# Output projection and feed-forward of the first graph layer, written out with two or three buffers and statistics made per group

## The reference, cut to what matters

```python
h_attn = (wV / (z + 1e-06)).reshape(N, D_MODEL)   # N = 6250, D_MODEL = 128, 8 heads
x = h_attn @ Wo.T + bo
x = h + x
x = _batch_norm(x, bn1_w, bn1_b)                  # mean and variance over the 6250 nodes
y = relu(x @ W1.T + b1) @ W2.T + b2               # 128 -> 256 -> 128
y = x + y
y = _batch_norm(y, bn2_w, bn2_b)
```

## Time and profile before

| | us |
|---|---|
| median of 3 runs | 5488.98 |
| lowest and highest of them | 5485.43, 5491.85 |
| the profiled execution, its own time | 5493.95 |
| span of its trace, first to last instruction | 5492.1 |
| from the first instruction of `attend_out` (1312.48) to the end of its groups (1378.3) | 65.8 |
| its statistics and scale (1379.1 to 1389.2) | 10.1 |
| from the first instruction of `feed_forward` (1390.50) to the end of its groups (1467.2) | 76.7 |
| its statistics and scale (1467.3 to 1477.3) | 10.1 |

### The profile page before, as it was taken

How to read it: one execution, slowest core, us unless ns; L and a number is a source line. 1 busy time by engine, 2 the same in 40 slices (tenths; PEclk the granted TensorE clock), 3 DMA queues, 4 the chain that set the end, 5 groups by cost and what they waited for, 6 DMA issues and landing times. The chain is left out here.

```text
span 5492.1 us, 99934 instructions
## 1 busy us (share of the span) xinstructions
PE 4376.5 (80%) x24072; PEld 3667.3 (67%) x24073; DVE 3581.9 (65%) x7941; ACT 2266.5 (41%) x4134; POOL 2777.4 (51%) x2730
## 2 busy tenths in 40 slices
PE   7566667666567777777648848999999999999998
PEld 4455555554234444444347738999999999999998
DVE  4888888886478888888786675444445654443444
ACT  0333443332135555555426644444444443344333
POOL 0477777773047777777412103444444443344433
PEclk8788888887887777877779959999999999999999
DMA  1444444442157777777425534343434442233332
GB/s 46 121 117 117 118 117 116 117 116 81 33 168 198 198 200 197 199 198 198 136 65 158 154 84 163 141 151 143 149 141 161 173 151 106 101 135 144 138 125 94
DMA packets 543152, 750.77 MB, mean 137 GB/s; under 512 B 57967, under 2 KB 441966, under 8 KB 542734
## 3 DMA queue, kind: packets, MB, share of 16 engines
q1 hardware_dynamic: 461182, 521.35, 28.4%
q0 software_dynamic: 81552, 224.63, 15.4%
HBM read 584.36 MB, written 161.41 MB: 136 GB/s over the span
## 5 line engine op out<-in xcount | busy, mean ns | idle before, releaser
L544 POOL DMA_INDIRECT arena<-table_kv,arena x1664 | 1732.7, 1041 | 653.1 <-issue 505.2
L2288 PE MATMUL ps<-moving,parts 128*128 128x384 f32 (+1 forms) x11662 | 2015.8, 331 | 38.5 <-ACT moving L2350 20.4
L2288 PEld LDWEIGHTS ps<-moving,parts 128*128 128x128 f32 x11662 | 1949.5, 188 | 72.1 <-ACT moving L2350 29.3
L2229 POOL CAST moving<-counts 128x1152 fp32r<-128x1152 uint8 (+1 forms) x420 | 476.2, 1134 | 737.9 <-PE ps L2288 606.4
L340 ACT ACTIVATE counted<-ps 128x392 uint8<-128x392 f32 x1568 | 665.0, 503 | 333.7 <-PE ps L331 300.3
L2229 POOL CAST moving<-big 128x1152 fp32r<-128x1152 uint8 (+1 forms) x413 | 468.6, 1135 | 610.1 <-PE ps L2288 610.1
L331 PE MATMUL ps<-by_place,by_lo 128*128 128x392 bf16 x1568 | 631.2, 525 | 105.3 <-DVE by_place L295 74.2
L654 PE MATMUL ps<-arena 128*128 128x137 f32 x1664 | 321.3, 349 | 344.6 <-DVE arena L788 332.5
L2350 ACT ACTIVATE moving<-counts 128x1152 fp32r<-128x1152 uint8 (+1 forms) x360 | 366.9, 1024 | 436.0 <-PE ps L2288 433.0
L2350 ACT ACTIVATE moving<-big 128x1152 fp32r<-128x1152 uint8 (+1 forms) x354 | 360.4, 1023 | 429.7 <-PE ps L2288 429.6
L654 PEld LDWEIGHTS ps<-arena 128*128 128x128 f32 x1664 | 273.1, 239 | 374.0 <-ACT arena L699 222.5
(11 more groups left out here) (329 smaller groups left out, 5337.3 us busy)
## 6 DMA issues: line engine op xcount, KB each, us to landing
counts<-adjacency SPq DMA_DIRECT2D x53, 2352.0 KB, 8.5
big<-adjacency SPq DMA_DIRECT2D x52, 2352.0 KB, 8.6
adjacency<-slots SPq DMA_DIRECT2D x784, 98.0 KB
edge_values<-arena SPq DMA_DIRECT2D x208, 256.0 KB
arena<-edge_values SPq DMA_DIRECT2D x208, 256.0 KB, 3.3
arena<-table_kv,arena POOLq DMA_INDIRECT x1664
big<-table_norm SPq DMA_DIRECT2D x60, 192.0 KB, 5.7
big<-adjacency SPq DMA_DIRECT2D x7, 1568.0 KB, 6.6
```

What stands on the lines that cost most here:

```text
L544: pool.indirect_dma_start(m.ring4[r][:, k * 2 * D:(k + 1) * 2 * D], None, table, bass.IndirectOffsetOnAxis(m.src[:, j * HALF + k:j * HALF ...
L2229: pool.tensor_copy(to, of).then_inc(by_pool, 1)
L2288: mm = pe.matmul(m.bank(g % 2, n * P), d.parts[SOURCE[u]][:, s + q, t_, :], moving[:, q * n * P:(q + 1) * n * P], start=(s + q == 0 and t_ ...
```

## The change

`attend_out` and `feed_forward` no longer loop on the engines: the 7 groups are written out.

In `attend_out`, weight sums get their 1e-6 and reciprocal in one instruction each for all 49 blocks (`z` now lies in `m.prod`). The input, the scaled rows, their transpose and both PSUM areas have two buffers each (group g uses banks 0 to 3 or 4 to 7). The multiplication (`weigh`) and the transposes (`turn`) of groups 0 and 1 are issued ahead of the loop, and those of group g+2 inside step g: on VectorE ahead of the wait for group g's product, on TensorE behind group g's product. The degrees move from behind the groups to between `weigh(1)` and step 0.

In `feed_forward` the normed input has three buffers, each half of the hidden layer two in SBUF (and one pair of banks in PSUM), the product two pairs of banks. ScalarE issues the norm of group g+2 behind the ReLU of group g; TensorE issues the hidden layer of group g+1 ahead of the product of group g; VectorE issues its ReLU of group g+1 ahead of the last step of group g.

`batch_stats` is split: `piece_stats` makes, behind each group's last step, the statistics of those 250-node pieces which that group completes (3, 4, 3, 4, 3, 4 and 4 of them), and `batch_scale` keeps the rest.

The diff, with removed lines left out where the kernel above shows them:

```diff
@@ -1413,14 +1413,28 @@
     act.activation(root, two[:, :, 1], ACT.Sqrt, bias=m.eps[:, 0:1]).then_inc(rooted, 1)
 
 
...
+PIECE = 250
+assert NODES % PIECE == 0
+def pieces(g):
+    return range(g * GN // PIECE, min((g + 1) * GN, NODES) // PIECE)
+def piece_stats(dve, m, g, done, stats):
+    six = m.small[:, 0:6 * (NODES // PIECE)].rearrange("p (b n) -> p b n", n=6)
+    dve.wait_ge(done, g + 1)
+    for b in pieces(g):
+        op = dve.bn_stats(six[:, b, :], m.feat[:, b * PIECE:(b + 1) * PIECE])
+    op.then_inc(stats, 1)
+def batch_scale(dve, m, stats, weight, bias, rooted, scaled):
+    dve.wait_ge(stats, GROUPS)
+    dve.bn_aggr(m.mean_var, m.small[:, 0:6 * (NODES // PIECE)]).then_inc(stats, 1)
     dve.wait_ge(rooted, 1)
     dve.reciprocal(m.scale, m.scale).then_inc(scaled, 1)
     dve.wait_ge(scaled, 1)
@@ -1433,102 +1447,150 @@
 
 def batch_root(act, m, stats, rooted):
 
...
+    act.wait_ge(stats, GROUPS + 1)
     act.activation(m.scale, m.mean_var[:, 1:2], ACT.Sqrt, bias=m.eps[:, 0:1]).then_inc(rooted, 1)
 
 
 def attend_out(nc, m, t):
 
 
...
+    with Phase(nc, "ao0", "x_in0 x_in1 added inverted weighed turned copied out done degs rooted2 stats rooted scaled") as (
+            block, x_in0, x_in1, added, inverted, weighed, turned, copied, out, done, degs, rooted2, stats, rooted, scaled):
+        x_in = (x_in0, x_in1)
+        x = [m.stage_c[:, k * GN:(k + 1) * GN] for k in range(2)]
+        mean = [m.stage_a, m.stage_b]
+        mean_t = [m.ring4[k][:, 0:GN] for k in range(2)]
+        sums = blocks(m.sums[:, 0:BLOCKS * A0], A0)
+        z = blocks(m.prod[:, 0:BLOCKS * H0], H0)
 
         @block.sync
         def _(sp):
...
+            for g in range(GROUPS):
+                wait(sp, done, g - 1)
+                sp.dma_start(x[g % 2], t["xT"][:, g * GN:(g + 1) * GN]).then_inc(x_in[g % 2], 16)
 
         @block.vector
         def _(dve):
...
+            def weigh(g):
+                wait(dve, turned, g - 1)
+                b = slice(g * GB, (g + 1) * GB)
+                dve.tensor_tensor(blocks(mean[g % 2]).rearrange("p b (n c) -> p b n c", c=C0),
+                                  sums[:, b, 0:D].rearrange("p b (n c) -> p b n c", c=C0), copies(z[:, b, :], 3, C0),
+                                  ALU.mult).then_inc(weighed, 1)
+            dve.tensor_scalar(z, sums[:, :, D:D + H0], 1e-6, None, ALU.add).then_inc(added, 1)
+            dve.wait_ge(added, 1)
+            dve.reciprocal(z, z).then_inc(inverted, 1)
+            dve.wait_ge(inverted, 1)
+            weigh(0)
+            weigh(1)
+            dve.tensor_scalar(m.degree[:, :], sums[:, :, A0 - 1], 1.0, None, ALU.add).then_inc(degs, 1)
             dve.wait_ge(rooted2, 1)
             dve.reciprocal(m.norm[:, :], m.norm[:, :]).then_inc(degs, 1)
...
+            for g in range(GROUPS):
+                if g + 2 < GROUPS:
+                    weigh(g + 2)
+                dve.wait_ge(out, g + 1)
+                dve.wait_ge(x_in[g % 2], 16 * (g // 2 + 1))
+                dve.scalar_tensor_tensor(m.feat[:, g * GN:(g + 1) * GN], m.ps[:, 2048 * (g % 2) + 1024:2048 * (g % 2) + 1024 + GN],
+                                         m.column["bo"], x[g % 2], ALU.add, ALU.add).then_inc(done, 1)
+                piece_stats(dve, m, g, done, stats)
+            batch_scale(dve, m, stats, m.column["n1w"], m.column["n1b"], rooted, scaled)
 
         @block.tensor
         def _(pe):
...
+            def turn(g):
+                pe.wait_ge(weighed, g + 1)
+                wait(pe, copied, g - 1)
+                turn_blocks(pe, m, 4 * (g % 2), mean[g % 2]).then_inc(turned, 1)
+            turn(0)
+            turn(1)
+            for g in range(GROUPS):
                 pe.wait_ge(copied, g + 1)
...
+                wait(pe, done, g - 1)
+                feature_product(pe, m, 4 * (g % 2) + 2, [(m.w["wo"][:, 0, :], mean_t[g % 2])]).then_inc(out, 1)
+                if g + 2 < GROUPS:
+                    turn(g + 2)
 
         @block.scalar
         def _(act):
...
+            def copy(g):
                 act.wait_ge(turned, g + 1)
...
+                wait(act, out, g - 1)
+                act.activation(mean_t[g % 2], m.ps[:, 2048 * (g % 2):2048 * (g % 2) + GN], ACT.Copy).then_inc(copied, 1)
+            copy(0)
             act.wait_ge(degs, 1)
...
+            act.activation(m.norm[:, :], m.degree[:, :], ACT.Sqrt).then_inc(rooted2, 1)
+            for g in range(1, GROUPS):
+                copy(g)
             batch_root(act, m, stats, rooted)
 
 
 def feed_forward(nc, m):
 
 
...
+    with Phase(nc, "ff0", "normed hidden0 hidden1 relu0 relu1 out done stats rooted scaled") as (
+            block, normed, hidden0, hidden1, relu0, relu1, out, done, stats, rooted, scaled):
+        x = [m.stage_a, m.stage_b, m.stage_d[:, 0:GN]]
+        act0 = [m.ring4[k][:, 0:GN] for k in (0, 1)]
+        act1 = [m.ring4[k][:, 0:GN] for k in (2, 3)]
 
         @block.scalar
         def _(act):
...
+            def norm(g):
+                wait(act, done, g - 2)
+                act.activation(x[g % 3], m.feat[:, g * GN:(g + 1) * GN], ACT.Identity,
                                bias=m.shift, scale=m.scale).then_inc(normed, 1)
...
+            norm(0)
+            norm(1)
+            for g in range(GROUPS):
+                act.wait_ge(hidden0, g + 1)
+                wait(act, out, g - 1)
+                act.activation(act0[g % 2], m.ps[:, 0:GN], ACT.Relu, bias=m.column["b1"][:, 0:1]).then_inc(relu0, 1)
+                if g + 2 < GROUPS:
+                    norm(g + 2)
             batch_root(act, m, stats, rooted)
 
         @block.tensor
         def _(pe):
...
+            def hidden(g):
                 pe.wait_ge(normed, g + 1)
...
+                wait(pe, relu0, g)
+                feature_product(pe, m, 0, [(m.w["w1"][:, 0, 0:P], x[g % 3])]).then_inc(hidden0, 1)
+                wait(pe, relu1, g)
+                feature_product(pe, m, 2, [(m.w["w1"][:, 0, P:2 * P], x[g % 3])]).then_inc(hidden1, 1)
+            hidden(0)
+            for g in range(GROUPS):
+                if g + 1 < GROUPS:
+                    hidden(g + 1)
                 pe.wait_ge(relu0, g + 1)
                 pe.wait_ge(relu1, g + 1)
...
+                wait(pe, done, g - 1)
+                feature_product(pe, m, 4 + 2 * (g % 2), [(m.w["w2"][:, 0, :], act0[g % 2]),
+                                                        (m.w["w2"][:, 1, :], act1[g % 2])]).then_inc(out, 1)
 
         @block.vector
         def _(dve):
...
+            def relu(g):
+                dve.wait_ge(hidden1, g + 1)
+                wait(dve, out, g - 1)
+                dve.tensor_scalar(act1[g % 2], m.ps[:, 1024:1024 + GN], m.column["b1"][:, 1:2], 0.0,
+                                  ALU.add, ALU.max).then_inc(relu1, 1)
+            relu(0)
+            for g in range(GROUPS):
+                if g + 1 < GROUPS:
+                    relu(g + 1)
                 dve.wait_ge(out, g + 1)
...
+                dve.scalar_tensor_tensor(m.feat[:, g * GN:(g + 1) * GN],
+                                         m.ps[:, 2048 + 1024 * (g % 2):2048 + 1024 * (g % 2) + GN],
+                                         m.column["b2"], x[g % 3], ALU.add, ALU.add).then_inc(done, 1)
+                piece_stats(dve, m, g, done, stats)
+            batch_scale(dve, m, stats, m.column["n2w"], m.column["n2b"], rooted, scaled)
 
 
 def project1(nc, m, t, table, x_table):
```

More of the change, by code:

```diff
@@ L1448, in _ @@
         @block.sync
         def _(sp):
-            with sp.Fori(0, GROUPS) as g:
-                sp.wait_ge(done, g + 1)
-                sp.dma_start(m.stage_c[:, 0:GN], t["xT"][:, ds(g * GN, GN)]).then_inc(loaded, 16)
+            for g in range(GROUPS):
+                wait(sp, done, g - 1)
+                sp.dma_start(x[g % 2], t["xT"][:, g * GN:(g + 1) * GN]).then_inc(x_in[g % 2], 16)
         @block.vector
         def _(dve):
[L1456 to L1466, removed]
-                dve.wait_ge(loaded, g * 16 + 16)
-                dve.scalar_tensor_tensor(m.feat[:, ds(g * GN, GN)], m.ps[:, 1024:1024 + GN], m.column["bo"],
-                                         m.stage_c[:, 0:GN], ALU.add, ALU.add).then_inc(done, 1)
@@ L1474, in _ @@
-            batch_stats(dve, m, stats, m.column["n1w"], m.column["n1b"], rooted, scaled)
+            for g in range(GROUPS):
[6 more added lines that the diff above has]
+                piece_stats(dve, m, g, done, stats)
@@ L1491, in _ @@
+            for g in range(1, GROUPS):
+                copy(g)
             batch_root(act, m, stats, rooted)
 def feed_forward(nc, m):
-    with Phase(nc, "ff0", "normed hidden relu0 relu1 out done stats rooted scaled") as (
-            block, normed, hidden, relu0, relu1, out, done, stats, rooted, scaled):
-        act0, act1 = m.stage_c[:, 0:GN], m.stage_c[:, GN:2 * GN]
+    with Phase(nc, "ff0", "normed hidden0 hidden1 relu0 relu1 out done stats rooted scaled") as (
[3 more added lines that the diff above has]
```

(19 more changed lines are left out.)

29 lines of the change are left out of this document (removed).

## The result

The changed kernel takes 5400.2 us (median of 4 runs, 5397.8 to 5411.8) against 5487.2 for the kernel before in the same series: 0.9839 of it, 95% interval 0.9825 to 0.9853. That is 87 us faster.

What follows compares the result with a forecast made beforehand. It took each group as a chain with one engine at work at a time. Gains of 43.1 (attend_out) and 31.8 (feed_forward), together 74.9, took 5493.95 to 5419.0; against the median, 4.97 lower, 5414.0 us, range 5403 to 5428.

Steps and rivals of the forecast that it cites:

- Start: attend_out: addition 0.55 and reciprocal 2.57 us for all blocks put the first scaling at 3.6 us, before 1.2.
- first last step: attend_out: DVE's last step of group 0 starts 11.2 us after the phase's start at 1312.48, between 10.5 and 11.5.
- rival 1: attend_out's clock stays at 1.2 GHz and PE is the bound: 42.5 in place of 31.6 us, 5425; chance 0.14.
- rival 3: attend_out: DVE holds each instruction until the one before leaves its pipe: 7.9 to 14.4 us more, 5422 to 5428; chance 0.03.
- 6 hidden layers and 7 products: 6 x 3.27 + 7 x 3.25 = 42.4: feed_forward: PE, the bound, runs these without stopping after its first 8 instructions, in 42.4 us.
- The first run of 8: feed_forward: PE's first 8 matrix instructions take 5.19 us, as in the kernel before.
- dip of the clock: feed_forward: 1.7 us taken off the gain of 33.5 for one dip of PE's clock, leaving 31.8.
- rival 2: feed_forward: PE still stops once per group for a late ReLU or norm: 9.3 us, 5423; chance 0.10.
- Nothing else: Rest of the kernel: no other gain or loss; scale chain stays, added semaphores cost nearest to 0.
- the spread of runs (3.5 down, 2.9 up): Whole kernel: run-to-run spread counted into the range, 3.5 us below and 2.9 above.
- Rival 4: Slower than before: moved code brings more stalls of PE's weight loads in score, 5520; chance 0.03.
- Transfers, degrees, semaphores: attend_out loads stay hidden, 0 to 0.3 us late; moved degrees take 0.8 off the path; both phases' semaphores cost near 0.

Runs made afterwards that it cites:

- e6: Changed kernel with the 25 statistics of each phase behind its groups, as before: 5406.4 us, attend_out 33.6 and feed_forward 54.7 to their aggregations.
- e7: Changed kernel with each statistics instruction made twice, the first result unused: 5410.6 us, attend_out 38.7 and feed_forward 50.0 to their aggregations.
- e18: Changed kernel with feed_forward's hidden layer of group g+1 behind the product of group g again: ratio 0.9860, feed_forward 59.5 us to its aggregation.
- e15: Changed kernel with 128 more VectorE instructions (waits long met) in feed_forward; the text gives no whole time.
- e14: Kernel before, unchanged, run beside itself: 5486.3 against 5495.0 us, ratio 0.9985.
- e1: Kernel before with 128 more TensorE instructions (waits long met) at the end of feed_forward; the text gives no whole time.
- e13: Kernel before with 64 more VectorE instructions (waits long met) at the start of feed_forward; the text gives no whole time.
- e3: attend_out as changed, feed_forward as in the kernel before: 5442.9 us, ratio 0.9914.
- e2: Changed kernel with 176 more TensorE instructions (waits long met) at the end of feed_forward: 5398 us less its 9.9 us of added waits.
- e8: Changed kernel with attend_out's reciprocals of groups 0 and 1 made first and weigh of groups 2 to 6 on GpSimd: 5398.1 us.

## Why the prediction was wrong, point by point

- *Direction, and what bounds each phase: right.* DVE sets `attend_out`, PE `feed_forward`; e6 and e7 show it by making VectorE's work less and more, e18 by putting PE's wait back.
- *attend_out: right.* 31.24 to the aggregation against 31.6. Start 3.2 against 3.6, first last step at t = 10.3 against 11.2, then 31.2 - 10.3 = 20.9 against 20.4, of which 0.43 is the wait in group 5. The clock was at 0.95 of full speed from 1318 to 1341, so rival 1 did not come. DVE's instructions overlapped by 0.08 (four statistics from 1325.05, the scaling at 1326.35), so rival 3 did not either.
- *feed_forward: the term that was mis-sized* is "6 hidden layers and 7 products: 6 x 3.27 + 7 x 3.25 = 42.4". These durations came from a PE that stood before each of them, and so hold the start and the end of each run. Back to back one takes 3.0 (6.01 for two): 39.1, so 3.3 less. The first run of 8 took 5.7 in place of 5.19, 0.5 more. The 1.7 us for a dip of the clock were not spent: PEclk is 0.98 from 1349 to 1390, and of 15 profiles with the changed phase only e15 has a dip, behind 6.87 us in which its added waits held PE. The old phase had 1, 0, 3, 4 and 2 dips in the five profiles with it (before, e14, e1, e13, e3), each a hidden layer of 4.7 to 5.0 us in place of 3.27 behind PE's stop of 2.6. So the gain in this phase is itself some us more or less by the execution that it is measured against. Nor did PE stop once per group (rival 2): 110 instructions ran without a gap. 51.4 + 0.5 - 3.3 = 48.6, as measured, and with the dip the gain there is 36.3 in place of 31.8. The Trainium skill, "TensorE: Matmul & The Clock Gate", section "Step-by-step: what each phase is for", says that a matmul by itself also pays for its drain, which a stream of them hides; the rows agree in kind, 3.25 apart against 3.0 in a stream.
- *The rest of the kernel: the step that failed* is "Nothing else", which put every other stage at no change, with a range that gave "the spread of runs (3.5 down, 2.9 up)" from three runs. Of the 13.8 us between 5414.0 and 5400.2, 1.8 are the lower median of the kernel before in this series, 5.1 the two phases, and some 7 the other stages. With 80.0 us from the phases alone, 5487.2 would be 5407, inside the range; what took it out lies in the other stages, above all in `score`: 8.3 us less in both copies of each kernel, because GpSimd's gathers there took 859 in place of 867 us. Rival 4 saw that the code of these stages would move and that `score` goes at GpSimd's pace, but it priced only stalls of PE, and only as a cost; the gathers themselves became shorter. Why they did is what the runs did not settle. The spread was too narrow as well: the kernel before has since run from 5477.2 to 5504.2, and its copies have medians of 5486.3 to 5495.0.
- *Two small readings* do not hold, and neither moves the forecast. Rival 1 prices a product at the lower clock at 3.27, which is eight instructions at the full one; four at the lower take 3.21. A load is due 5.5 us after it leaves, not 5.7, by the prediction's own terms.
- *Transfers, degrees, semaphores: right.* The degrees cost DVE 3.24 us of waiting, all of it before product 0 was ready. The last step of group 5 waited for its product, not for its load.

## What to carry to other kernels

Where a loop hands one group from engine to engine and the busiest of them works little more than half the time (54% and 63% here), write it out with two buffers and a group ahead; with the statistics and the joined reciprocals that gave 39 of 43.5 us in `attend_out`. Then find the engine that is now the bound. The second group ahead brought 4.6 us more there, and statistics made per group only 2.3, because the bounding engine makes them; in `feed_forward`, where another engine is the bound, they brought 6.0. Price an engine that becomes the bound by its stream, not by durations taken between waits. Read a gain of under ten us in a kernel of 5 ms from the stage's own trace: the total moved by 8.7 us between two copies of one program. And when a stage that was not touched changes, look first at the engine that paces it: `score` followed GpSimd's gathers, not the packets that were suspected.

## What the runs showed of the hardware that was not expected

- Waits that are long met are not free on a busy path: 176 instructions of them behind TensorE's last product put off the next phase by 9.9 us (e2, 96.2 against 86.3). From that product's end to the next phase's first instruction it took 16.2 us in place of 6.0, so each wait took between 56 and 92 ns. Where TensorE had 12 us to spare, 128 of them cost nothing (e1, 3.36 us from its aggregation to the next phase as before).
- GpSimd multiplies 128x896 float32 values in 1.70 us beside a busy VectorE, and VectorE's own 1.15 us do not change (e8).
- A TensorE loop of about 1590 instructions had 9 packets of 16 KB per pass in the kernel before, none behind the first pass in the changed kernel, and in e2 and e13 some passes with and some without. 128 instructions more ahead of it ended them (e1). No time could be tied to that.
- The same 827 gathers of GpSimd took 854.6 to 873.4 us over 20 profiles, with the same median of 0.95 us, and the stage that they pace took 255 to 256 us more than they did each time.
- In `feed_forward` with a stop of 2.6 us in each group, TensorE's granted clock fell to 0.50 up to four times in a phase; with none, or with one of 1.29 us per group (e18), it stayed at 1.00 once it had risen.
